# A mixture of experts in a fused last stage: gate and up with the weights stationary, router weights carried through memory

## The chip, the cores and the metric

The kernel runs on one core of a Trainium2 chip. The metric is device time in microseconds of one execution; the figure compared is the median of several runs. A core has five engines with queues of their own: TensorE (PE in the profile, its weight loads PEld), VectorE (DVE), ScalarE (ACT), GpSimd (POOL) and SyncE (SP), which here only issues DMAs. Each engine works through its own instruction queue in order and waits there for semaphores.

## The reference

Two layers of gated cross-attention and mixture of experts, on 32 sequences (B) of 256 tokens (S) with 256 features (D). The change lies in the second layer's mixture, the last part of the computation:

```python
# hidden_states: layernorm of the sequence, [B, 256, 256]; E = 8 experts, the first 4 with an MLP of I = 128
scores = sigmoid(x @ Wr)
_, idx = top_k(scores + router_bias, 2)
w = take_along_axis(scores, idx); w = w / (sum(w) + 1e-9)
cw = zeros((T, 8)).at[arange(T)[:, None], idx].add(w)
g = einsum('th,ehi->tei', x, Wg)
u = einsum('th,ehi->tei', x, Wu)
hid = silu(g) * u
mlp_out = einsum('tei,eih->teh', hid, Wd)
routed = einsum('te,teh->th', cw[:, :4], mlp_out)
routed += cw[:, 4:5] * x + cw[:, 6:7] * x + cw[:, 7:8] * relu(x)
shared = depthwise causal convolution of 4 taps over the sequence
return routed + shared        # then x + tanh(g_ffn[1]) * this
```

Everything is float32. Products that need it are split into a high and a low plane of a faster 32-bit format and run in three passes (`PASSES`: high by high, high by low, low by high); `split_product` writes them out.

## The kernel before

The program has stages: the first layer's attention, its routing and experts, and the last stage, the function `finish`, in which the change lies. `finish` works on one sequence of 256 tokens at a time, `b` in 0 to 31, as a software pipeline over steps `s` = 2 to 36. In step `s` the engines work on several batches at once: the gather and sum of the first layer's answers for batch `s` (`combine_first`, `combine_second`), the second layer's attention of `s - 2`, the norm and router of `s - 3`, the experts of `s - 4`, the closing sum of `s - 5`. Each engine has a function `step(s, p)`, in which the order of its work is written out by hand; nothing is reordered at run time, and semaphores named after what is ready (`hid_ok`, `total_ok`) tie the engines together. `at_least(eng, sem, n)` is the wait that protects a buffer from being overwritten early. `by_itself` puts an instruction of its own between waits.

The experts of one batch before the change. The 256 tokens are two tiles of 128 (`i` = 0, 1). PE makes `gates[i]` and `ups[i]` (`gate_up`) with the tokens of the tile as the stationary operand and the weights of the four experts (4 x 128 = 512 columns) moving, so the result has tokens on the partitions. ACT's `tanh` and DVE's `silu` make `hs`. DVE's `weigh` multiplies, in one fused operation for each expert, `hs` by the token's router weight, a scalar for each partition `cw[:, p, i, e]`, and by `ups`. PE turns the result (`turn_hid`, four transposes for each `i`), into the bank of `gates[i]`, since `down` needs the hidden features on the partitions. ACT's `hidden_turned` copies the high plane out, DVE's `hidden_low` makes the low plane, and PE's `down` sums the experts into `total`. `add_rest` adds the convolution `cv`, and DVE's `close` makes the output.

PE's order within step `s` before: `gate_up(s-4, 1, 0)`, `turn_c`, `down(s-5, 1)`, `values`, `add_rest(s-5, 1)`, `turn_hid(s-4, 0)`, `turn3`, `keys`, `gate_up(s-4, 1, 1)`, `turn4(s-3)`, `queries`, `turn_k`, `down(s-4, 0)`, `context`, `gate_up(s-3, 0, 0)`, `logits`, `attended`, `gate_up(s-3, 0, 1)`, `turn_hid(s-4, 1)`, `output`, `add_rest(s-4, 0)`. `gate_up(s-4, 1, 0)` waits, for the bank of `gates[1]`, until `hidden_low(s-5, 1)` is done.

DVE's order before: `weigh(s-4, 0)`, `stat4(s-3)`, `values_out`, `normalise4(s-3)`, `close(s-5)`, `hidden_low(s-4, 0)`, `key_max`, `silu(s-4, 1)`, four operations of `convolve`, `x4_lower(s-3)`, two more of `convolve`, `relu`, `own_heads`, `weigh(s-4, 1)`, `silu(s-3, 0)`, then `route_and_combine`: fifteen small router operations of batch `s-3` (semaphore `route`), between which stand `combine_first` and `combine_second` of batch `s`, `hidden_low(s-4, 1)` and `x3_new(s-2)`.

POOL's order: `shares(s-4)` (which waits for all of `route`), `keep_x2(s-2)` (it writes `f_x2k`), `norm4(s-3)` (which waits for `stat4` and writes `f_var`, `f_rs`), the gathers for batch `s`, `add_relu`, `norm3`. DVE's `normalise4` waits for `f_rs`.

The names in the profile carry the prefix `f_` for tiles of this stage. The lines that matter: L80 is every product of `split_product`, told apart by its tile; L2386 is `turn_hid`, L2379 `add_rest`, L2130 `weigh`, L2185 `hidden_low`, L2022 `hidden_turned`, L2179 `silu`, L2202 `x4_lower`, L2161 `normalise4`, L2153 `close`, L2197 `convolve`, L1930 `keep_x2`, L1939 and L1942 `norm4`, L1955 `shares`.

Of the kernel before, what the change touches and what calls it, by code (L numbers as in the profile page):

```python
# [31 lines left out]
P = 128  # L32
# [1726 lines left out]
def finish(nc, t, keep):  # L1759
# [4 lines left out]
    with ctx:  # L1764
# [8 lines left out]
        def sem(name):  # L1773
# [39 lines left out]
        cw = sb("f_cw", [P, 2, QT, E1])  # L1813
# [6 lines left out]
        hs = sb("f_hs", [P, QT, EM * P])  # L1820
        hid = sb("f_hid", [P, QT, EM * P])
        hidT = sb("f_hidT", [P, 2, QT, EM, P], F32R)
# [25 lines left out]
        hidT_low = [sem(f"f_hidT_low{i}") for i in range(QT)]  # L1848
        gate_made, up_made, th_ok, hs_ok, hid_ok, hid_made, hidT_ok, down_made, total_ok, yo_ok = (
            [sem(f"f_{s}{i}") for i in range(QT)] for s in (  # L1850
                "gate_made", "up_made", "th_ok", "hs_ok", "hid_ok", "hid_made", "hidT_ok", "down_made", "total_ok",
                "yo_ok"))
        yo_ok = yo_ok[0]
# [16 lines left out]
        def weight2(name, plane, k):  # L1870

            base = LATE_AT[name] - LATE_AT["Wg"]
            both = halves[:, plane, base:base + EM * KD * P].rearrange("p (e k i) -> p e k i", e=EM, k=KD)
            return both[:, :, k]

# [22 lines left out]
        @block.sync  # L1898
        def _(eng):
            def store(b, p):  # L1900
                eng.wait_ge(yo_ok, b + 1)
                eng.dma_start(t["out"][bass.ds(b, 1)].rearrange("o (k p) d -> p (o k) d", p=P), yo[:, p]) \
                    .then_inc(yo_out[p], 16)

            early["load_x1"](eng, 2, 0)

            def step(s, p):
                if live(s + 1):
                    early["load_x1"](eng, s + 1, 1 - p)
                if live(s):  # L1910
                    early["load_ctx"](eng, s, p)
                if live(s - 5):
                    store(s - 5, 1 - p)

            all_steps(eng, step)
            for p in range(2):
                eng.wait_ge(yo_out[p], 16 * (B // 2))

        @block.gpsimd
        def _(eng):  # L1920
# [26 lines left out]
            def shares(b, p):  # L1947


                eng.wait_ge(route, N_ROUTE * (b + 1))  # L1950
                eng.wait_ge(rg4_ok, b + 1)
                at_least(eng, x3p_ok, QT * b)
                at_least(eng, x4r_ok, QT * b)
                by_itself(eng, waited)
                nc.gpsimd.tensor_tensor(own[:, 0], cws[:], rg4[:], ALU.mult).then_inc(own_ok, 1)  # L1955
                nc.gpsimd.tensor_tensor(own[:, 3], cw[:, p, :, EM + 3], keep["gate"][:, 3:4].to_broadcast([P, QT]),
                                        ALU.mult).then_inc(own_ok, 1)
# [29 lines left out]
        def _(eng):  # L1987
# [23 lines left out]
            def first_tap(b):  # L2011

                eng.wait_ge(x4p_ok, b + 1)
                at_least(eng, total_ok[1], b)
# [70 lines left out]
            def step(s, p):  # L2085
# [6 lines left out]
                if live(s - 4):  # L2092
                    tanh(s - 4, 1)
                    first_tap(s - 4)
                    hidden_turned(s - 4, 0)
# [10 lines left out]
                if live(s - 3):  # L2106
                    x4_padded(s - 3)
                if live(s - 2):
                    queries_out(s - 2)
# [5 lines left out]
                if live(s - 4):  # L2115
                    hidden_turned(s - 4, 1)
# [4 lines left out]
        def _(eng):  # L2121
            def weigh(b, p, i):

                eng.wait_ge(hs_ok[i], b + 1)
                eng.wait_ge(up_made[i], b + 1)
                eng.wait_ge(route, N_ROUTE * (b + 1))
                at_least(eng, hid_made[i], b)
                for e in range(EM):
                    es = slice(e * P, (e + 1) * P)
                    nc.vector.scalar_tensor_tensor(hid[:, i, es], hs[:, i, es], cw[:, p, i, e:e + 1], ups[i][:, es],  # L2130
                                                   ALU.mult, ALU.mult).then_inc(hid_ok[i], 1)
# [16 lines left out]
            def close(b, p):  # L2148

                eng.wait_ge(total_ok[1], b + 1)  # L2150
# [31 lines left out]
            def hidden_low(b, i):  # L2182

                eng.wait_ge(hidT_ok[i], b + 1)
                nc.vector.scalar_tensor_tensor(hidT[:, 1, i], gates[i][:].rearrange("p (e s) -> p e s", e=EM), 0.5,  # L2185
                                               hidT[:, 0, i].bitcast(F32), ALU.mult, ALU.subtract) \
                    .then_inc(hidT_low[i], 1)
# [40 lines left out]
            def route_and_combine(b, p, c, cp):  # L2228
# [13 lines left out]
                at_least(eng, own_ok, N_OWN * b)  # L2242
                chain(nc.vector.tensor_scalar(re[:], re[:], 1.0, None, ALU.add))
# [31 lines left out]
                chain(nc.vector.tensor_tensor(cw[:, p], oh[:, :, 0], oh[:, :, 1], ALU.add))  # L2275
# [3 lines left out]
                chain(nc.vector.tensor_tensor(cw[:, p], cw[:, p], rsg[:], ALU.mult))  # L2279
# [3 lines left out]
                chain(nc.vector.reduce_sum(cws[:], cw[:, p], AX.X))  # L2283
# [7 lines left out]
                chain(nc.vector.tensor_tensor(cw[:, p], cw[:, p], wide(cws[:]), ALU.mult))  # L2291
                wait_chain()
                chain(nc.vector.tensor_tensor(cws[:], cw[:, p, :, EM], cw[:, p, :, EM + 2], ALU.add))
# [10 lines left out]

            def step(s, p):
                q = 1 - p
                if live(s - 4):
                    weigh(s - 4, p, 0)
# [14 lines left out]
                if live(s - 4):  # L2323
                    hidden_low(s - 4, 0)
                if live(s - 2):
                    key_max(s - 2)
                if live(s - 4):
                    silu(s - 4, 1)
                    convolve(s - 4, 1, KC - 1)
                if live(s - 3):  # L2330
                    x4_lower(s - 3)
                if live(s - 4):
                    convolve(s - 4, KC - 1, KC)
# [3 lines left out]
                if live(s - 4):  # L2337
                    weigh(s - 4, p, 1)
# [13 lines left out]
        def _(eng):  # L2352
# [8 lines left out]
            def down(b, i):  # L2361
                eng.wait_ge(hidT_low[i], b + 1)
                if i == 0:
# [3 lines left out]
                split_product(nc, total[:, i * D:(i + 1) * D], lambda a, e: hidT[:, a, i, e],  # L2367
                              lambda a, e: wd2[:, a, e], EM, stop=False).then_inc(down_made[i], 1)
# [5 lines left out]
            def add_rest(b, i):  # L2374

                if i == 0:
                    eng.wait_ge(cv_ok, N_CV * (b + 1))
                for k in range(KD):
                    last = nc.tensor.matmul(total[:, i * D + k * P:i * D + (k + 1) * P], cv[:, k, i * P:(i + 1) * P],  # L2379
                                            ident[:], is_transpose=True, start=False, stop=k == KD - 1)  # L2380
                last.then_inc(total_ok[i], 1)

            def turn_hid(b, i):
                eng.wait_ge(hid_ok[i], EM * (b + 1))
                for e in range(EM):
                    last = nc.tensor.transpose(gates[i][:, e * P:(e + 1) * P], hid[:, i, e * P:(e + 1) * P], ident[:])  # L2386
                last.then_inc(hid_made[i], 1)
# [46 lines left out]
            def gate_up(b, i, which):  # L2434

                out, name, done = ((gates, "Wg", gate_made), (ups, "Wu", up_made))[which]
                if which == 0:
                    eng.wait_ge(x4T_low, b + 1)
                    at_least(eng, hidT_low[i], b)
                else:  # L2440
                    at_least(eng, hid_ok[i], EM * b)
# [30 lines left out]
            def step(s, p):  # L2472
# [9 lines left out]
                if live(s - 5):  # L2482
                    add_rest(s - 5, 1)
                if live(s - 4):
                    turn_hid(s - 4, 0)
# [10 lines left out]
                if live(s - 4):  # L2496
                    down(s - 4, 0)
# [9 lines left out]
                if live(s - 4):  # L2507
                    turn_hid(s - 4, 1)
                if live(s - 2):
                    output(s - 2)  # L2510
                if live(s - 4):
                    add_rest(s - 4, 0)
# [4 lines left out]
def build(nc, t):  # L2517

    with ExitStack() as ctx:
# [24 lines left out]
        keep["w1_loaded"] = ctx.enter_context(nc.semaphore("w1_loaded"))  # L2544
        routing(nc, t, keep, ctx)
# [72 lines left out]
```

## Time and profile before

| | us |
|---|---|
| median of 3 runs | 2226.85 (2221.72 to 2227.82) |
| span of the profiled execution | 2225.1 |
| what the median lies above that span | 1.75 |
| busy in the whole span: PE, DVE, ACT, POOL | 2186.7, 1728.1, 1282.0, 645.1 |
| busy in 100 us of the last stage (1800 to 1900): PE, DVE, ACT, POOL | 100.00, 90.05, 55.85, 57.71 |

The last stage begins at about 1592 us; its steps 4 to 33 lie between 1631 and 2189 us. PE's busy time is modelled from the ends of pipelined matmuls, so a stretch in which PE is 100% busy can hold short waits. In the timelines an operation's length overlaps the next one's start a little, on DVE by some 0.08 us; what an operation costs in a row of others is the distance of the starts.

### The profile page before, as it was taken

The page shows a single profiled execution, that of the slowest core. Times are in us where ns is not written, and L with a number is a line of the kernel's source. Part 1 is how long each engine was busy: PE and PEld are TensorE (multiplying, and loading weights), DVE is VectorE, ACT ScalarE, POOL GpSimd, SP SyncE. Part 2 cuts the span into 40 slices and gives each one's busy share as a digit, 9 for nine tenths or more (in the row PEclk, how much of TensorE's full clock was granted, in tenths as well). Part 3 has the DMA queues.
Part 4 walks back from the last instruction along what each step waited for, and adds up shares of the span by engine and source line. Part 5 has one row for each costly group of instructions (what it writes and reads, how often), then busy time and mean ns, then how long its engine had stood idle before and what let it go on. Part 6 is the DMA issues. An engine that isn't in the chain of part 4 may idle for free. (4 is left out here: it accounts for less than half of the span.)

```text
span 2225.1 us, 48355 instructions
## 1 busy us (share of the span) xinstructions
PE 2186.7 (98%) x15486; PEld 1865.5 (84%) x15486; DVE 1728.1 (78%) x6112; ACT 1282.0 (58%) x3251; POOL 645.1 (29%) x1162
## 2 busy tenths in 40 slices
PE   8999999999999999999999999999999999999997
PEld 6777777777777777777699999999878888888886
DVE  6788888888888888888675555555579999999986
ACT  6776776776776776776443333433345555555553
POOL 1123223222232232232220000000355555555541
PEclk9999999999999999999899999999999999999999
DMA  5320110110110110110052222221212222222210
GB/s 189 124 97 22 37 40 23 37 39 21 40 38 20 39 39 20 40 32 27 11 161 73 81 86 72 81 77 41 89 58 65 65 65 64 65 65 65 65 39 20
DMA packets 111642, 129.57 MB, mean 58 GB/s; under 512 B 14898, under 2 KB 98089, under 8 KB 111264
## 3 DMA queue, kind: packets, MB, share of 16 engines
q1 hardware_dynamic: 98249, 105.06, 14.9%
q0 software_dynamic: 12288, 21.21, 3.3%
q8 instruction: 128, 2.10, 0.4%
q14 instruction: 122, 1.00, 0.1%
q10 hardware_dynamic: 855, 0.19, 0.0%
HBM read 84.26 MB, written 54.53 MB: 62 GB/s over the span
## 5 line engine op out<-in xcount | busy, mean ns | idle before, releaser
L711 ACT ACTIVATE a_prob<-a_prob,a_nmax 128x376 f32<-128x376 f32 x512 | 309.7, 606 | 155.3 <-DVE a_nmax L857 155.3
L1457 ACT ACTIVATE e_hidden<-e_first,keep_b 128x256 f32<-128x256 f32 x320 | 134.1, 471 | 283.3 <-PE e_first L80 282.8
L857 DVE CUSTOM_DVE_ANT_0 a_prob<-a_score,a_mask_row 128x376 f32<-128x376 f32 x512 | 266.6, 540 | 10.8 <-issue 5.6
L80 PE MATMUL e_second<-e_w,e_hidden 128*128 128x256 f32 x1920 | 239.5, 284 | 0.0
L80 PEld LDWEIGHTS e_second<-e_w,e_hidden 128*128 128x128 f32 x1920 | 232.6, 192 | 0.0
L869 DVE TENSOR_SCALAR a_prob<-a_prob,a_rden 128x376 f32<-128x376 f32 x512 | 220.9, 453 | 2.5
L1151 PE MATMUL a_turned<-keep_ident,a_prob 128*128 128x128 f32 (+1 forms) x1536 | 217.3, 277 | 2.8 <-DVE a_probT L876 1.6
L1151 PEld LDWEIGHTS a_turned<-keep_ident,a_prob 128*128 128x128 f32 (+1 forms) x1536 | 173.5, 142 | 43.5 <-issue 27.6
L1142 PE MATMUL a_score<-a_kT,a_qT 64*128 64x376 f32 x1024 | 196.4, 502 | 0.0
L876 DVE COPY a_probT<-a_turned 128x384 f32<-128x384 f32 x256 | 139.8, 546 | 54.4 <-PE a_turned L1151 54.4
L719 ACT ACTIVATE a_probT<-a_turned 128x384 f32<-128x384 f32 x256 | 124.9, 488 | 92.1 <-PE a_turned L1151 91.7
L177 POOL TENSOR_SCALAR r_var<-r_mv 128x2 f32<-128x2 f32 x64 | 12.2, 190 | 562.9 <-issue 501.2
L201 POOL DMA_INDIRECT slots<-r_x2h,r_sidx x128 | 134.4, 1050 | 77.0 <-DVE keep_row L332 46.5
L80 PE MATMUL a_work<-a_wkv,a_kvin 128*128 128x512 f32 (+1 forms) x576 | 154.3, 403 | 1.4 <-DVE a_att L881 1.4
L1178 PE MATMUL a_work<-a_probT,a_vo 128*64 128x256 f32 (+1 forms) x1152 | 148.4, 393 | 2.6 <-ACT r_rT L217 1.9
L1695 POOL DMA_INDIRECT w_in<-answers,o_row x128 | 132.9, 1038 | 58.7 <-issue 31.0
L1178 PEld LDWEIGHTS a_work<-a_probT,a_vo 128*64 128x64 f32 (+1 forms) x1152 | 75.4, 138 | 81.6 <-issue 50.2
L1504 DVE CAST e_hidden<-e_hidden 128x512 fp32r<-128x512 f32 x160 | 68.5, 428 | 96.8 <-ACT e_hidden L1457 96.6
L1142 PEld LDWEIGHTS a_score<-a_kT,a_qT 64*128 64x128 f32 x1024 | 88.1, 186 | 50.4 <-issue 18.4
L1690 POOL COPY o_row<-keep_row 128x4 uint32<-128x4 uint32 x32 | 10.0, 313 | 412.3 <-DMA answers<-e_y 412.3
L80 PEld LDWEIGHTS a_work<-a_wkv,a_kvin 128*128 128x128 f32 (+1 forms) x576 | 101.6, 186 | 20.8 <-issue 1.5
L80 PE MATMUL e_first<-e_rowsT,keep_w 128*128 128x256 f32 x960 | 118.8, 282 | 0.0
(237 smaller groups left out, 5231.1 us busy)
## 6 DMA issues: line engine op xcount, KB each, us to landing
w_in<-W SPq DMA_DIRECT2D x32, 512.0 KB, 4.1
slots<-a_zeros SPq DMA_DIRECT2D x8, 1280.0 KB, 8.7
keep_rows<-slots SPq DMA_DIRECT2D x40, 256.0 KB, 3.9
answers<-e_y SPq DMA_DIRECT2D x40, 256.0 KB, 2.2
a_xn<-x SPq DMA_DIRECT2D x32, 256.0 KB, 2.9
a_xr<-x SPq DMA_DIRECT2D x32, 256.0 KB, 3.8
x<-r_x SPq DMA_DIRECT2D x32, 256.0 KB, 4.0
w_in<-x SPq DMA_DIRECT2D x32, 256.0 KB, 2.6
```

The costliest lines, as they stand in the source:

```text
L80: last = nc.tensor.matmul(out, stationary(a, t), moving(b, t), start=start and n == 0, stop=stop and n == len(todo) - 1)
L201: nc.gpsimd.indirect_dma_start(out=t["slots"], out_offset=bass.IndirectOffsetOnAxis(ap=sidx[:, p, n:n + 1], axis=0), in_=x2h[:, p, n // 2] ...
L711: nc.scalar.activation(prob[:, u % 4, a], prob[:, u % 4, a], ACT.Exp, bias=nmax[:, u % 4, a:a + 1], scale=-1.0, accum_out=den[:, u % 4, a: ...
L719: nc.scalar.activation(probT[:, u // 2 % 2, a, :, u % 2 * P:(u % 2 + 1) * P], turned_keys[a], ACT.Copy) \
L857: nc.vector.tensor_tensor_reduce(prob[:, u % 4, a], score[SCORE_AT[u][a]][:, 0:NKV], mask_row[:, p], -1.0, 3.0e38, ALU.add, ALU.min, nmax[ ...
L869: nc.vector.tensor_scalar(prob[:, u % 4, a], prob[:, u % 4, a], rden[:, u % 4, a:a + 1], None, ALU.mult) \
L876: nc.vector.tensor_copy(probT[:, u // 2 % 2, a, :, u % 2 * P:(u % 2 + 1) * P], turned_keys[a]) \
L1142: nc.tensor.matmul(score[SCORE_AT[u][a]][:, 0:NKV], qT[rows, p, m, i * P:(i + 1) * P], kT[rows, p, m], start=True, stop=True).then_inc(sco ...
L1151: last = nc.tensor.transpose(turned_keys[a][0:hi - lo, j], prob[:, u % 4, a, lo:hi], ident[:])
L1178: last = nc.tensor.matmul(out[64 * a:64 * a + 64, 0:S], vo[0:hi - lo, p, j, m, a], probT[0:hi - lo, m % 2, a, j], start=j == 0, stop=j == 2)
L1457: nc.scalar.activation(hidden[:, 2 * j + i], first[:, j, i * CH:(i + 1) * CH], ACT.Relu, bias=b1[:, 2 * j + i, bass.ds(e, 1)]).then_inc(re ...
L1695: nc.gpsimd.indirect_dma_start(out=picked[p][:, n], out_offset=None, in_=t["answers"][0:rows], in_offset=bass.IndirectOffsetOnAxis(ap=row[ ...
```

## The change

Gate and up are made with the weights as the stationary operand and all 256 tokens moving, so their results have the hidden features on the partitions, and the tiles are now pairs of experts (`j` = 0, 1; `gates[j]` and `ups[j]` hold two experts of 256 tokens). The transposes `turn_hid` fall away. A token's router weight is then no longer a scalar for each partition: the weights are turned by DVE in blocks of 32, written to a DRAM tensor `chosen` by four small stores, and read back by one DMA that gives every partition all 1024 of them (`cw_wide`). `weigh` becomes `share_ups` (up times router weight) and `hidden` (times `hs`). `down` sums by expert pairs, `add_rest` comes in one piece.

```diff
+        cwp = sb("f_cwp", [P, 2, 32])
+        cw = [cwp[:, n, 0:QT * E1].rearrange("p (e i) -> p i e", i=QT) for n in range(2)]
+        cw_rows = sb("f_cw_rows", [P, 32])
+        cw_wide = sb("f_cw_wide", [P, EM, S])
...
+            def spread_weights(b):                      # SP, first in step s, for b = s - 4
+                eng.wait_ge(cw_turned, b + 1)
+                for g in range(0, P, 32):
+                    eng.dma_start(t["chosen"][:, g:g + 32], cw_rows[g:g + EM * QT]).then_inc(cw_out, 16)
+                eng.wait_ge(cw_out, 16 * 4 * (b + 1))
+                at_least(eng, share_ok[1], b)
+                eng.dma_start(cw_wide[:].rearrange("p e s -> p (e s)"),
+                              t["chosen"].rearrange("c q -> (c q)").partition_broadcast(P)).then_inc(cw_in, 16)
...
-            def hidden_turned(b, i):                    # ACT
-                eng.wait_ge(hid_made[i], b + 1)
-                at_least(eng, down_made[i], b)
-                nc.scalar.activation(hidT[:, 0, i], gates[i][:].rearrange("p (e s) -> p e s", e=EM), ACT.Copy,
-                                     scale=0.5).then_inc(hidT_ok[i], 1)
+            def hidden_high(b, j):
+                eng.wait_ge(hid_ok[j], b + 1)
+                at_least(eng, down_made[j], b)
+                nc.scalar.activation(hid2[:, 0, pair(j)], hid[:, j].rearrange("p (e s) -> p e s", e=2), ACT.Copy,
+                                     scale=0.5).then_inc(hid_high[j], 1)
...
-            def weigh(b, p, i):                         # DVE
-                eng.wait_ge(hs_ok[i], b + 1)
-                eng.wait_ge(up_made[i], b + 1)
                 eng.wait_ge(route, N_ROUTE * (b + 1))
-                at_least(eng, hid_made[i], b)
-                for e in range(EM):
-                    es = slice(e * P, (e + 1) * P)
-                    nc.vector.scalar_tensor_tensor(hid[:, i, es], hs[:, i, es], cw[:, p, i, e:e + 1], ups[i][:, es],
-                                                   ALU.mult, ALU.mult).then_inc(hid_ok[i], 1)
+                at_least(eng, cw_out, 16 * 4 * b)       # weights_turned(b, p)
+                nc.vector.transpose(cw_rows[:], cwp[:, p]).then_inc(cw_turned, 1)
+
+            def share_ups(b, j):
+                eng.wait_ge(up_made[j], b + 1)
+                eng.wait_ge(cw_in, 16 * (b + 1))
+                at_least(eng, hid_low[j], b)
+                nc.vector.tensor_tensor(hid[:, j].rearrange("p (e s) -> p e s", e=2),
+                                        ups[j][:].rearrange("p (e s) -> p e s", e=2), cw_wide[:, pair(j)],
+                                        ALU.mult).then_inc(share_ok[j], 1)
+
+            def hidden(b, j):
+                eng.wait_ge(hs_ok[j], b + 1)
+                eng.wait_ge(share_ok[j], b + 1)
+                nc.vector.tensor_tensor(hid[:, j], hs[:, j], hid[:, j], ALU.mult).then_inc(hid_ok[j], 1)
...
+            def down(b, j):                             # PE
+                eng.wait_ge(hid_low[j], b + 1)
+                for i in range(QT):
+                    for n, (a, c, e) in enumerate((a, c, 2 * j + e) for e in range(2) for a, c in PASSES):
+                        last = nc.tensor.matmul(total[:, i * D:(i + 1) * D], hid2[:, a, e, i * P:(i + 1) * P],
+                                                wd2[:, c, e], start=j == 0 and i == 0 and n == 0, stop=False,
+                                                skip_group_check=True)
...
             def gate_up(b, j, which):
                 if which == 0:
                     eng.wait_ge(x4T_low, b + 1)
-                    at_least(eng, hidT_low[i], b)
+                    at_least(eng, hs_ok[j], b)
                 else:
-                    at_least(eng, hid_ok[i], EM * b)
-                split_product(nc, out[i][:].rearrange("p (e i) -> p e i", e=EM),
-                              lambda a, k: x4T[:, a, k, i * P:(i + 1) * P],
-                              lambda a, k: weight2(name, a, k), KD).then_inc(done[i], 1)
+                    at_least(eng, share_ok[j], b)
+                for e in range(2):
+                    last = split_product(nc, out[j][:, e * S:(e + 1) * S], lambda a, k: weight2(name, a, k)[:, 2 * j + e],
+                                         lambda a, k: x4T[:, a, k], KD)
```

The notes behind `#` in this diff name the engine or the function; they are not in the code. The orders after the change, where they differ:

- DVE: `weights_turned(s-4)` stands where `weigh(s-4, 0)` stood. `hidden_low(s-4, 0)` leaves its place before `key_max`. `share_ups(s-4, 0)` stands behind the four operations of `convolve` and before `x4_lower`, `hidden(s-4, 0)` behind `x4_lower`. Where `weigh(s-4, 1)` stood come `share_ups(s-4, 1)`, `hidden(s-4, 1)` and `hidden_low(s-4, 0)`. `hidden_low(s-4, 1)` stays among the router's operations. The last of these writes the weights into `cwp`, which DVE clears once at the start of the stage.
- ACT: `hidden_high(s-4, 0)` stands behind `x4_padded` (`hidden_turned(0)` stood behind `first_tap`), `hidden_high(s-4, 1)` at the end.
- PE: no `turn_hid`; `down(s-4, 0)` at the end of the step, behind `output`, instead of between `turn_k` and `context`; `add_rest(s-5)` in one piece where `add_rest(s-5, 1)` stood.
- SP: `spread_weights(s-4)` ahead of `load_x1(s+1)`, `load_ctx(s)` and `store(s-5)`.

## Rows read from the trace of the kernel before

**Rows 1.** The page, busy time of each engine over the whole span.

```profile
PE 2186.7 (98%) x15486; PEld 1865.5 (84%) x15486; DVE 1728.1 (78%) x6112; ACT 1282.0 (58%) x3251; POOL 645.1 (29%) x1162
```

**Rows 2.** Chain of waits, last stage: start, length (us), what.

```profile
2116.59 0.19 POOL f_var L1939
...
2132.55 0.61 DVE f_hidT L2185
```

**Rows 3.** Timeline of PE: start, length, line, tile, count [idle before].

```profile
1908.85 1.62 PE L80 MATMUL f_gates<-late,f_x4T 128*128 128x512 f32 x6
...
1910.44 1.68 PE L80 MATMUL f_total<-f_wd,f_hidT 128*128 128x256 f32 x12
...
1913.04 0.60 PE L2386 MATMUL f_gates<-keep_ident,f_hid 128*128 128x128 f32 x4
1913.47 0.60 PE L2394 MATMUL f_bank_x<-keep_ident,f_x3h 128*128 128x128 f32 x4
...
2133.30 1.62 PE L80 MATMUL f_gates<-late,f_x4T 128*128 128x512 f32 x6 [2.19 <-DVE f_hidT L2185]
...
2151.78 1.62 PE L80 MATMUL f_gates<-late,f_x4T 128*128 128x512 f32 x6
...
2170.22 1.63 PE L80 MATMUL f_gates<-late,f_x4T 128*128 128x512 f32 x6
...
2217.66 2.93 PE L80 MATMUL f_total<-f_wd,f_hidT 128*128 128x256 f32 x12 [0.98 <-DVE f_hidT L2185]
```

**Rows 4.** Timeline of DVE: one steady step, and the last batch's first `weigh`.

```profile
1892.09 1.12 DVE L2130 SCALAR_TENSOR_TENSOR f_hid<-f_hs,f_cw,f_ups 128x128 f32<-128x128 f32 x4 [0.21 <-DVE f_cws L2293]
...
1895.80 0.74 DVE L2161 TENSOR_SCALAR f_x4h<-f_x,f_mv,f_rs 128x256 f32<-128x256 f32 x2 [0.84 <-POOL f_rs L1942]
...
1900.63 0.68 DVE L2202 TENSOR_TENSOR f_x4T<-keep_bank,f_x4T 128x512 fp32r<-128x512 f32 x1
1901.23 0.86 DVE L2197 SCALAR_TENSOR_TENSOR f_cv<-f_x4p,o_conv_w,f_cv 128x256 f32<-128x256 f32 x2
...
1903.32 1.11 DVE L2130 SCALAR_TENSOR_TENSOR f_hid<-f_hs,f_cw,f_ups 128x128 f32<-128x128 f32 x4
1904.35 0.68 DVE L2179 SCALAR_TENSOR_TENSOR f_hs<-f_th,f_gates 128x512 f32<-128x512 f32 x1
...
1910.57 1.12 DVE L2130 SCALAR_TENSOR_TENSOR f_hid<-f_hs,f_cw,f_ups 128x128 f32<-128x128 f32 x4 [0.21 <-DVE f_cws L2293]
...
2206.04 1.12 DVE L2130 SCALAR_TENSOR_TENSOR f_hid<-f_hs,f_cw,f_ups 128x128 f32<-128x128 f32 x4 [0.23 <-DVE f_cws L2293]
```

**Rows 5.** Timeline of POOL in the same step.

```profile
1892.08 0.20 POOL L1955 TENSOR_TENSOR f_own<-f_cws,f_rg 128x2 f32<-128x2 f32 x1 [4.54 <-DVE f_cws L2293]
...
1892.92 1.28 POOL L1930 TENSOR_TENSOR f_x2k<-w_in,o_bo 128x512 f32<-128x512 f32 x1
1894.52 0.19 POOL L1939 TENSOR_SCALAR f_var<-f_mv 128x2 f32<-128x2 f32 x1 [0.32 <-DVE f_mv L2141]
```

**Rows 6.** Timeline of DVE in the stage of the experts.

```profile
1121.67 0.43 DVE L1504 CAST e_hidden<-e_hidden 128x512 fp32r<-128x512 f32 x1 [0.28 <-ACT e_hidden L1457]
1122.13 0.69 DVE L1506 TENSOR_TENSOR e_hidden<-e_hidden 128x512 fp32r<-128x512 f32 x1
```

**Rows 7.** Timeline of SP's queue: issues in a row.

```profile
1128.22 0.47 SPq L1403 DMA_DIRECT2D late<-WkT  x1
1128.73 0.47 SPq L1403 DMA_DIRECT2D late<-WvT  x1
```

**Rows 8.** DMA issues: count, KB each, median us from issue to landing.

```profile
w_in<-W SPq DMA_DIRECT2D x32, 512.0 KB, 4.1
...
out<-f_yo SPq DMA_DIRECT2D x32, 256.0 KB, 2.2
...
r_slot<-slot SPq DMA_DIRECT2D x1, 128.0 KB, 6.7
a_go<-g_o SPq DMA_DIRECT2D x1, 128.0 KB, 6.4
```

More of the change, by code:

```diff
@@ L1955, in shares @@
                 nc.gpsimd.tensor_tensor(own[:, 0], cws[:], rg4[:], ALU.mult).then_inc(own_ok, 1)
-                nc.gpsimd.tensor_tensor(own[:, 3], cw[:, p, :, EM + 3], keep["gate"][:, 3:4].to_broadcast([P, QT]),
+                nc.gpsimd.tensor_tensor(own[:, 3], cw[p][:, :, EM + 3], keep["gate"][:, 3:4].to_broadcast([P, QT]),
                                         ALU.mult).then_inc(own_ok, 1)
@@ L2107, in step @@
                     x4_padded(s - 3)
+                if live(s - 4):
+                    hidden_high(s - 4, 0)
                 if live(s - 2):
@@ L2115, in step @@
                 if live(s - 4):
-                    hidden_turned(s - 4, 1)
+                    hidden_high(s - 4, 1)
             all_steps(eng, step)
@@ L2274, in route_and_combine @@
                 wait_chain()
-                chain(nc.vector.tensor_tensor(cw[:, p], oh[:, :, 0], oh[:, :, 1], ALU.add))
+                chain(nc.vector.tensor_tensor(cw[p], oh[:, :, 0], oh[:, :, 1], ALU.add))
                 if low:
@@ L2278, in route_and_combine @@
                 wait_chain()
-                chain(nc.vector.tensor_tensor(cw[:, p], cw[:, p], rsg[:], ALU.mult))
+                chain(nc.vector.tensor_tensor(cw[p], cw[p], rsg[:], ALU.mult))
                 if combining:
@@ L2302, in x3_new @@
                                                keep["gate"][:, 1:2], x2k[:], ALU.mult, ALU.add).then_inc(x3_ok, 1)
+            nc.vector.memset(cwp[:], 0.0).then_inc(cw_set, 1)
             def step(s, p):
@@ L2329, in step @@
                     convolve(s - 4, 1, KC - 1)
+                    share_ups(s - 4, 0)
                 if live(s - 3):
@@ L2332, in step @@
                 if live(s - 4):
+                    hidden(s - 4, 0)
                     convolve(s - 4, KC - 1, KC)
@@ L2337, in step @@
                 if live(s - 4):
-                    weigh(s - 4, p, 1)
+                    share_ups(s - 4, 1)
+                    hidden(s - 4, 1)
+                    hidden_low(s - 4, 0)
                 if live(s - 3):
@@ L2372, in values, with add_rest @@
                 product(bank_c[0:C, 0:D], lambda k: cT[:, k], lambda k: weight("WvT", k), KD).then_inc(v_made, 1)
[L2374 to L2387, printed above, removed]
+            def add_rest(b):
+                eng.wait_ge(cv_ok, N_CV * (b + 1))
+                for i in range(QT):
+                    for k in range(KD):
+                        last = nc.tensor.matmul(total[:, i * D + k * P:i * D + (k + 1) * P],
+                                                cv[:, k, i * P:(i + 1) * P], ident[:], is_transpose=True, start=False,
+                                                stop=i == QT - 1 and k == KD - 1, skip_group_check=True)
+                last.then_inc(total_ok, 1)
             def turn3(b):
@@ L2432, in context, with gate_up @@
                 last.then_inc(cx_made, 1)
-            def gate_up(b, i, which):
+            def gate_up(b, j, which):
                 out, name, done = ((gates, "Wg", gate_made), (ups, "Wu", up_made))[which]
@@ L2482, in step @@
                 if live(s - 5):
-                    add_rest(s - 5, 1)
-                if live(s - 4):
-                    turn_hid(s - 4, 0)
+                    add_rest(s - 5)
                 if live(s - 2):
@@ L2511, in step @@
                 if live(s - 4):
-                    add_rest(s - 4, 0)
+                    down(s - 4, 0)
             all_steps(eng, step)
```

65 lines of the change are left out of this document (31 added, 34 removed).

## Prediction

> **What bounds the kernel now.** I read the page's busy shares first. TensorE (PE) shows 98% [rows 1], which suggests that any PE work taken away is time gained. The chain of waits says otherwise. In the piece of it that lies in the last stage it runs through a whole step on VectorE (DVE), goes through GpSimd's (POOL) variance instructions and comes back to DVE [rows 2]. It reaches PE only from `hidden_low` (L2185). So I went to the timelines of a steady step.
>
> PE's next `gate_up` cannot start before DVE has made the low half of the previous batch. When DVE was held up once, PE stood idle for 2.19 us with exactly that releaser [rows 3]. DVE's step, from one first `weigh` to the next, is 1910.57 - 1892.09 = 18.48 us [rows 4]. PE's own step is shorter. It shows where DVE has no gather left to combine: 2170.22 - 2151.78 = 18.44 us [rows 3]. PE therefore looks full because its own length happens to be 0.04 us under DVE's. In a steady step DVE waits for nothing that PE makes: it stands before `weigh` for its own router result, and 0.84 us before `normalise4` for POOL's `rs4` [rows 4]. **DVE, with POOL in its loop, sets the pace, and PE is close behind.**
>
> **The change, part by part.**
>
> *PE.* The two `turn_hid` go: 1913.47 - 1913.04 = 0.43 us each, 0.86 per step. Gate and up become 12 products of 256 columns instead of 6 of 512. `down` already is twelve of 256: 1.68 us beside 1.62 for a gate group of six [rows 3], so four groups cost 4 x 0.06 = 0.24 more. PE's own work falls by about 0.6 us to some 17.8. `down(0)` used to stand between `turn_k` and `context` and covered ScalarE's (ACT) copy of the keys. Now PE must wait for that copy, under 1 us. All of this lies beside DVE's longer step and is worth nothing on the path. If DVE weren't the limit, the 0.6 would come off each step and the wait would give it back. `add_rest` in one piece costs the same four transposes; `total` is ready early for `close`.
>
> *ACT.* `hidden_high` is the same 128x512 copy as `hidden_turned`. It moves in the queue behind `x4_padded`, ahead of `queries_out`; DVE feeds it 0.6 us after the operation that feeds `x4_padded`, so what waits behind it (`queries_out`, `tanh(0)`) is late by about one such copy, which DVE's longer stretch before `silu(0)` covers.
>
> *DVE, busy.* Out: eight `weigh` operations of 128x128, in two groups of 1904.35 - 1903.32 = 1.03 us each, -2.06. In: two `share_ups` and two `hidden`, each a tensor_tensor of 128x512. The row of that kind in this stage, `x4_lower` with one operand in PSUM, takes 1901.23 - 1900.63 = 0.60 us start to start [rows 4]; with both operands in SBUF it is as long, 0.69 for one [rows 6]. Four make +2.40. `hidden(1)` directly follows `share_ups(1)`, on which it depends. A dependent pair starts 0.03 us after the first has ended (1121.67 + 0.43 to 1122.13, [rows 6]), instead of overlapping it by 0.08: +0.11. `hidden_low` reads SBUF instead of PSUM and stays at 0.61 [rows 2]. In sum 2.40 + 0.11 - 2.06 = +0.45. The reason: one fused operation with three operands becomes two with two, so twice the elements pass.
>
> The Trainium skill ("VectorE: DVE Perf Modes", Rules for kernel authors) advises to minimize the number of operations. By that rule, taken by itself, eight becoming four would halve the 2.06 to 1.03, and the sum of all would end near 2227. The rows go the other way, since the elements outweigh the starts saved: 2.06 against 2.40.
>
> *DVE, where the first group stood.* The first `weigh` stood between the router and `stat4`. The transpose of 128x32 that takes its place has no row; it lies between nothing and one 128x512 operation (0.69), and either is hidden, for this reason: `normalise4` waits for POOL, and POOL's variance instruction stands in POOL's queue behind `shares` and `keep_x2`, which start at the router's end. POOL starts `shares` at 1892.08 and `keep_x2` at 1892.92, which takes 1.28 and ends at 1894.20. Today the variance starts at 1894.52 [rows 5]. With `stat4` a microsecond earlier, POOL can start it only at about 1894.2, so `normalise4` moves from 3.71 us after the step's start (1895.80 - 1892.09) to about 3.40. Of 1.03 us removed here only 0.31 is gained; the remaining 0.72 becomes a longer wait for POOL. Bounds: 0.2 (POOL needs the same latency again) and 1.03 (POOL is not in the way).
>
> *One step then:* +2.40 + 0.11 - 1.03 (second group) - 0.31 (first group) = **+1.17 us**, 19.65 in place of 18.48. Bounds by the ends above: +0.45 and, with 0.69 for each of the four, +1.64.
>
> *The router weights through memory.* They travel: transpose on DVE, four stores by SyncE (SP), a wait, one broadcast of 512 KB, and `share_ups(0)` waits for it. The slot of `share_ups(0)` is that of today's `x4_lower` (1900.63 - 1895.80 = 4.83 us behind `normalise4`), less the `hidden_low(0)` that leaves this stretch (0.6), so 3.40 + 4.83 - 0.60 = 7.63 us after the step's start. SP issues in a row start 0.51 us apart [rows 7]; the fourth starts at 0.2 + 1.53 = 1.73. A store lands in at most 2.2 us (256 KB), a 512 KB load in 4.1 [rows 8]. Upper end: 1.73 + 2.2 + 4.1 = 8.0; lower, if a small store took nothing, 5.8. For stores this small I take 1.7, so 7.5: just in time, with 0.1 us per step set aside for gathers on the same engines. A broadcast reads one place 128 times; the nearest rows, a broadcast and a plain load of 128 KB side by side at the start, took 6.4 and 6.7 us [rows 8], so it isn't slower by itself. Behind SP's two waits stand `load_x1`, `load_ctx` and `store`. They leave some 4 us into the step; the loads are used one or two steps later, and the `yo` buffer is two deep, so nobody waits.
>
> *Ends.* 28 steps (4 to 31, as long as there is something to combine) bear the full sum. In steps 32 and 33 DVE is lighter and PE sets the pace; its gain of 0.6 and its new wait cancel: 0. Step 34 bears the DVE sum without POOL's part: +1.5. In the last batch the broadcast is not covered: `share_ups(0)` at 7.5, then seven DVE operations of some 0.6 to 0.8 up to the last low half at about 12.5, two `down` as long as today's last one (2.93 us after a gap, [rows 3]), `add_rest`, `close` and the store: about 23 us, where today it is 19.1 from 2206.04 [rows 4] to the span's end at 2225.1: +4. The tail: +5 (1.5 to 6). The single stall of 2.19 us came by a late gather, which has more time now: -1. The memset of `cwp`, once: nothing.
>
> *Sum:* 28 x (1.17 + 0.1) = 35.6; + 5 - 1 = +39.6. Span 2225.1 + 39.6 = 2264.7 us. The median of the runs (2226.85) lies 1.75 above the profiled span; within the rounding of my terms I say **2265**.
>
> **The rivals.**
>
> *A, PE sets the pace (other side).* For it: the 98%. Against it: the 2.19 us wait and 18.44 under 18.48. It would need DVE's new step to be under PE's 17.8, so 1.9 us less than my sum. Then 30 steps x 0.6 to 0.75 come off, and the tail gives some back: about 2207.
>
> *B, the broadcast is late.* Its landing decides, from 7.63 us on; each microsecond later costs 28 us. At 9 us: 2264 + 36 = 2300. For it: only 0.1 us of margin, and gathers run at that time. Against it: the rows' upper end is 8.0 (+10 us).
>
> *C, POOL is not in the way.* The first `weigh` counts in full: +0.45 per step, 28 x 0.45 + 4 = +17: 2242.
>
> *D, nothing measurable.* DVE's two groups of two large operations cost no more than the eight small ones did, so that only POOL's wait and the tail are left, and both are small: 2227. For it: the number of operations falls by half. Against it: 0.60 for one large operation beside 1.03 for four small ones [rows 4]. The Trainium skill's rule above ends here.
>
> **How the numbers follow.** My case 0.52, B (2275 or more) 0.20, C 0.11, A 0.09, D 0.08. My own case lies within 2250 to 2275. The range for 8 in 10 takes in C and the larger part of B: 2238 to 2297. A measurement here can tell about 0.3% (7 us): faster 0.10, same 0.07, slower 0.83.
>
> **What would show it.** Right: a DVE step of 19.5 to 19.8 us; PE with waits of half a microsecond before `context`, `gate_up(0)` and `attended`, busy some 90%; an `f_x4h` wait for `f_rs` that has grown above 1 us; `share_ups(0)` with little wait for the DMA. Wrong: a DVE that waits for PE (A), an `f_x4h` wait no longer than before (C), a wait of a microsecond or more at `share_ups(0)` (B), or tensor_tensors much under 0.6 us.

## The result and the profile after

The changed kernel takes **2267.18 us** (median of 4 runs, 2263.54 to 2272.03) beside 2227.25 us (four runs) of the kernel before on the same chip: a ratio of 1.0182 [1.0164, 1.0200], so 40 us or 1.8% slower. The forecast was 2265. The profiled execution is the longest of the four: it took 2272.03 us, its span is 2270.2, so its sum stands some 5 us above the median.

The page's busy line of the changed kernel, over the whole span:

```profile
PE 2191.1 (97%) x15998; PEld 1891.2 (83%) x15998; DVE 1745.8 (77%) x6017; ACT 1271.8 (56%) x3251; POOL 678.7 (30%) x1162
```

The busy times in a stretch of the last stage (start and end; length; busy us of PE, its weight loads, DVE, ACT and POOL; then the granted clock, the DMA share and GB/s):

```profile
1800.00:1900.00 100.00, 92.71 (x661) 85.50 (x660) 86.80 (x292) 48.15 (x116) 57.88 (x96) 1.00 0.29 88
```

Against [rows 1], where PE had 98%, nothing seems to have moved. In the stretch PE went from 100.00 to 92.71 and DVE from 90.05 to 86.80: both are less busy, in a step that is longer. So there are waits. The two lists of waits (waiting engine, tile and line; releaser; us in total, times, longest), from 1750 to 2100:

```profile
DVE f_v L2174 <- PE f_bank_c L1886: 19.0, 18, 1.1
DVE f_x4h L2189 <- POOL f_rs L1959: 16.3, 18, 1.1
...
DVE f_hid L2151 <- issue: 0.8, 3, 0.4
...
PE f_bank_c L1886 <- ACT f_kp L2066: 8.5, 18, 0.5
PE keep_bank L1886 <- ACT f_x4p L2072: 7.1, 17, 0.4
PE f_bank_x L1886 <- ACT f_qT L2079: 4.8, 17, 0.3
PE f_gates L80 <- DVE f_x4T L2230: 2.7, 7, 0.6
```

PE waits before `context` and `attended`, as forecast, before `gate_up(0)` in 7 of 18 steps, and also before `logits`, which the forecast didn't name. DVE waits 0.9 us for POOL's `f_rs`, about as long as before ([rows 4], 0.84), and now 1.1 us for PE's `values` ahead of it. At `share_ups(0)` (L2151) it hardly waits for the broadcast: three times in 18 steps, by 0.4 us at most. The list gives these three as `issue`; each ends 0.1 us after a late broadcast has landed.

The timeline of DVE in one undisturbed step, the counterpart of [rows 4], then POOL's of the same step, the counterpart of [rows 5], then SP's queue:

```profile
1772.30 0.21 DVE L2144 STREAM_TRANSPOSE f_cw_rows<-f_cwp 128x32 f32<-128x32 f32 x1
...
1774.66 0.42 DVE L2174 TENSOR_TENSOR f_v<-f_bank_c,o_bv 120x256 f32<-120x256 f32 x1 [1.10 <-PE f_bank_c L1886]
1775.97 0.74 DVE L2189 TENSOR_SCALAR f_x4h<-f_x,f_mv,f_rs 128x256 f32<-128x256 f32 x2 [0.89 <-POOL f_rs L1959]
...
1780.19 0.68 DVE L2151 TENSOR_TENSOR f_hid<-f_ups,f_cw_wide 128x512 f32<-128x512 f32 x1
1780.79 0.68 DVE L2230 TENSOR_TENSOR f_x4T<-keep_bank,f_x4T 128x512 fp32r<-128x512 f32 x1
1781.39 0.68 DVE L2159 TENSOR_TENSOR f_hid<-f_hs,f_hid 128x512 f32<-128x512 f32 x1
1781.99 0.88 DVE L2225 SCALAR_TENSOR_TENSOR f_cv<-f_x4p,o_conv_w,f_cv 128x256 f32<-128x256 f32 x2
...
1784.08 0.68 DVE L2151 TENSOR_TENSOR f_hid<-f_ups,f_cw_wide 128x512 f32<-128x512 f32 x1
1784.86 0.69 DVE L2159 TENSOR_TENSOR f_hid<-f_hs,f_hid 128x512 f32<-128x512 f32 x1
1785.47 0.68 DVE L2213 SCALAR_TENSOR_TENSOR f_hid<-f_hid 128x512 fp32r<-128x512 f32 x1
...
1792.13 0.21 DVE L2144 STREAM_TRANSPOSE f_cw_rows<-f_cwp 128x32 f32<-128x32 f32 x1
```

```profile
1772.47 0.20 POOL L1972 TENSOR_TENSOR f_own<-f_cws,f_rg 128x2 f32<-128x2 f32 x1 [5.01 <-DVE f_cws L2323]
...
1773.32 1.28 POOL L1947 TENSOR_TENSOR f_x2k<-w_in,o_bo 128x512 f32<-128x512 f32 x1
1774.68 0.19 POOL L1956 TENSOR_SCALAR f_var<-f_mv 128x2 f32<-128x2 f32 x1
...
1783.55 1.27 POOL L1984 TENSOR_TENSOR f_x3p<-f_x3p,f_x4r 128x512 f32<-128x512 f32 x1 [0.60 <-DVE f_x4r L2238]
```

```profile
1772.54 1.29 SPq L1916 DMA_DIRECT2D chosen<-f_cw_rows  x4
1774.71 0.35 SPq L1919 DMA_DIRECT2D f_cw_wide<-chosen  x1
```

DVE's step is 1792.13 - 1772.30 = **19.83 us** in place of 18.48: +1.35. The four new operations cost 0.60, 0.60, 0.78 and 0.61 us from start to start, 2.59 in sum, for the 2.06 of the eight removed. POOL's variance (L1956) comes right behind `keep_x2`, without the idle time of [rows 5]. From POOL's first `shares` to `normalise4` it is 1775.97 - 1772.47 = 3.50 us, where it was 1895.80 - 1892.08 = 3.72 [rows 4, 5]. So of the 1.03 us taken away ahead of `stat4`, 0.22 came through. 2.59 - 1.03 - 0.22 = 1.34: the step is explained.

### The profile page after: what moved, and what is told of

Same layout as the page of the kernel before. It is cut to its first block and busy times, and to the rows that moved or that the text cites. A ratio compares the mean times of both kernels' runs of the same rounds, so it can differ in the third digit from the quotient of the medians.

```text
span 2270.2 us, 49509 instructions
## 1 busy us (share of the span) xinstructions
PE 2191.1 (97%) x15998; PEld 1891.2 (83%) x15998; DVE 1745.8 (77%) x6017; ACT 1271.8 (56%) x3251; POOL 678.7 (30%) x1162
## 5 line engine op out<-in xcount | busy, mean ns | idle before, releaser
L1695 POOL DMA_INDIRECT w_in<-answers,o_row x128 | 147.2, 1150 | 58.7 <-issue 30.7
L2403 PE MATMUL f_total<-f_wd,f_hid 128*128 128x256 f32 x768 | 113.0, 298 | 6.9 <-DVE f_hid L2213 6.9
```

The costliest lines, as they stand in the source:

```text
L1695: nc.gpsimd.indirect_dma_start(out=picked[p][:, n], out_offset=None, in_=t["answers"][0:rows], in_offset=bass.IndirectOffsetOnAxis(ap=row[ ...
```

## The experiments

Each ratio is against the kernel before on the same chip. Steps are distances of DVE's starts in undisturbed steps.

**Who sets the pace.** `e3_no_share` takes the two `share_ups` out of the changed kernel.

```diff
-                    share_ups(s - 4, 0)
...
-                    share_ups(s - 4, 1)
                     hidden(s - 4, 1)
...
-                nc.vector.tensor_tensor(hid[:, j], hs[:, j], hid[:, j], ALU.mult).then_inc(hid_ok[j], 1)
+                nc.vector.tensor_tensor(hid[:, j], hs[:, j], ups[j][:], ALU.mult).then_inc(hid_ok[j], 1)
```

> The changed kernel without the two share_ups: hidden multiplies hs by ups straight from PSUM, so the router weights are left out of the sum; the trip through memory and the wait for it stay. Theory (DVE sets the pace): two operations of 0.60 us and the dependent wait of 0.19 go, the step becomes 18.45 us, 28 x 1.39 = 39 us less, about 2228, unless PE with its new waits becomes the limit on the way, at 18.5 to 19 us (2230 to 2244). Rival (PE sets the pace): unchanged, 2267.

Measured: 2226.33 us, ratio 1.0002 [0.9992, 1.0012], some 40 us below the changed kernel, though PE's work and the trip through memory are left in. So the loss hangs on DVE's work. Its lists of waits, same columns and stretch as above:

```profile
DVE f_v L2176 <- PE f_bank_c L1886: 35.0, 19, 1.9
...
PE f_bank_c L1886 <- ACT f_kp L2066: 9.0, 19, 0.5
```

The step is 18.48. DVE now waits 1.8 us for PE in each step (35.0 in 19), and PE hardly for anything but ACT's key copy: PE sets the pace there, with some 18.0 of its own and 0.47 of that wait. That this equals the step before is chance, and it puts a floor under the change that the forecast's rival A, with 2207, didn't have.

`e4_before_pe`, `e5_before_dve` and `e6_before_both` relieve the kernel before of PE work, of DVE work, and of both:

```diff
-                split_product(nc, out[i][:].rearrange("p (e i) -> p e i", e=EM),       # e4, e6
...
+                todo = [(a, c, k) for k in range(KD) for a, c in PASSES[:2]]
...
-        N_CV = KD * (KC - 1)                                                           # e5, e6
+        N_CV = KD * (KC - 2)
...
-                    convolve(s - 4, KC - 1, KC)
```

> The kernel before with two of the three passes of gate and up; the third, low by high, is left out. PE's work falls by 8 products of 512 columns, 1.85 us per step; DVE's work is the same. Theory (DVE sets the pace at 18.48): the steps stay, steps 32 and 33 and the tail give 4 to 7 us, 2220 to 2223. Rival (PE sets the pace at 98% busy): 30 x 1.85 = 55 us less, 2172.

> The kernel before without the last tap of its convolution, which is left out: VectorE has two operations of 128x256 fewer per step, some 0.8 us; TensorE has the same work. Theory (VectorE 18.48 and TensorE 18.44 are within 0.04 of each other, so relief of one alone gives nothing): 2220 to 2225 us. Rival (VectorE alone sets the pace, with TensorE's 18.44 containing waits that shrink): 28 x 0.8 = 22 us less, 2203.

> The kernel before with both reliefs: the last tap of the convolution and the third of the three passes of the gate and up products are left out, so VectorE has 0.8 us less per step and TensorE 1.85. Theory: the step falls to VectorE's 17.7, 28 x 0.8 = 22 us and some 4 at the ends: 2197 to 2203. Rival (something third, ScalarE or the DMA, holds the step at 18.4): 2218 to 2225.

Measured: 2222.52 (0.9989 [0.9976, 1.0002], step 18.48), 2220.95 (0.9971 [0.9960, 0.9981], step 18.44) and 2207.27 (0.9903 [0.9886, 0.9919], steps of 17.7 to 18.3). 1.85 us less PE work gives nothing in a step, 0.8 less DVE work gives the 0.04 by which DVE was longer (28 x 0.04 = 1 us; the other 5 I didn't follow), and only both together shorten the step. The tie of [rows 3, 4] is real. The last gain is 20 us where I had 24 to 30, since the step came down only here and there to 17.7; what held the others I didn't follow.

**The trip through memory.** `e2_no_trip` leaves out the turning, the stores, the broadcast and the wait for it.

```diff
-                if live(s - 4):
-                    spread_weights(s - 4)
...
-                eng.wait_ge(cw_in, 16 * (b + 1))
+                eng.wait_ge(cw_set, 2)
```

> The changed kernel without the trip of the router weights through memory: cw_wide is set to one once, SP sends nothing for it, so the router weights are left out of the sum over the experts; all of PE's and DVE's work stays (the transpose too). Theory (DVE's own operations make the step, the trip is nearly covered): the steps stay at 19.83, only the few late broadcasts (2.4 us in all) and 2 to 4 us of the tail come off, 2260 to 2264. Rival (the trip or its 512 KB on the DMA engines make the step longer): 20 us or more come off, 2245 or less.

Measured: 2262.96 (1.0176 [1.0158, 1.0194]). By the ratios this is 1.3 us below the changed kernel, within the intervals, and an undisturbed step is 19.81 in place of 19.83. The trip is nearly covered: the broadcast is issued 2.41 us behind the transpose and takes 4.3 (median), so it lands 6.7 behind, 1.2 ahead of `share_ups(0)` at 7.89. In the three steps with a wait it was issued 2.9 to 3.5 behind and landed 8.0 to 8.3 behind.

**The wait for POOL.** If `keep_x2` holds `norm4` back, swapping them should give the step 0.9 us.

```diff
-                if live(s - 2):
-                    keep_x2(s - 2, p)
                 if live(s - 3):
                     norm4(s - 3)
+                if live(s - 2):
+                    keep_x2(s - 2, p)
```

> The changed kernel with norm4 ahead of keep_x2 in POOL's order; nothing is left out. Theory (DVE sets the pace, and the place of the first weigh is lost to a wait for POOL's norm behind keep_x2): f_var starts about 1.1 us earlier, the step falls from 19.83 by 0.7 to 0.9 us, so 28 x 0.8 = 22 us less than the changed kernel, about 2245. Rival (PE's new waits for ACT set the step): the step stays at 19.8, about 2267.

Measured: 2273.33 (1.0216 [1.0199, 1.0233]), step 19.91: a miss for the theory. DVE's and POOL's timelines of `e1_norm_first`:

```profile
1773.79 0.21 DVE L2144 STREAM_TRANSPOSE f_cw_rows<-f_cwp 128x32 f32<-128x32 f32 x1
...
1776.56 1.70 DVE L2189 TENSOR_SCALAR f_x4h<-f_x,f_mv,f_rs 128x256 f32<-128x256 f32 x2
...
1776.75 1.35 POOL L1947 TENSOR_TENSOR f_x2k<-w_in,o_bo 128x512 f32<-128x512 f32 x1
```

`normalise4` has no wait ahead of it any more and starts 2.77 us behind the transpose instead of 3.67, 0.90 earlier. But its two operations take 1.70 us instead of 0.74: they run into `keep_x2` and get done about when it is. To tell this from a limit of PE, `e7_x2_last` put `keep_x2` behind `add_relu`, and `e10_x2_dve` gave it to DVE:

```diff
-                    keep_x2(s - 2, p)                  # POOL; norm4 follows shares
...
+                    keep_x2(s - 2, p)                  # e7: POOL, behind add_relu; e10: DVE, ahead of values_out
```

> The kernel after, with GpSimd's order changed: norm4 directly behind shares, and the 128x512 addition keep_x2 moved behind the gather and add_relu, so that it runs neither ahead of f_var nor beside the normalise4 operations. Nothing is left out. Theory (the wait for f_rs costs the step 0.9 us; the run with norm4 ahead of keep_x2 lost its gain because the two normalise4 operations stood beside keep_x2, 1.70 us against 0.74): normalise4 starts 2.8 us behind the transposes instead of 3.67 and takes 0.74; DVE's step falls from 19.83 to about 18.95, some 28 x 0.9 = 25 us: 2242 us, 2238 to 2252. Rival (TensorE's order and its waits for ScalarE, 17.8 of its own and 1.2 of waits, hold the step as well): the step stays above 19.5 and the time above 2258.

> The kernel after, with keep_x2 (the 128x512 addition of the bias to x2) taken from GpSimd and given to VectorE, right ahead of f_v, where VectorE waits 1.1 us for TensorE; norm4 then follows shares directly. Nothing is left out. Theory (in the kernel after, keep_x2 holds norm4 back, and wherever else GpSimd ran it, one of VectorE's operations stood beside it for 1.0 us; on VectorE it is some 0.6 us in a hole of 1.1): normalise4 starts 2.8 us behind the transposes instead of 3.67 and takes 0.74; the step falls from 19.83 to about 19.0; 28 x 0.85 = 24 us: 2243 us, 2238 to 2255, the upper end if the broadcast, which lands 6.7 us behind the transposes, is now waited for before share_ups(0), at 7.0. Rival (TensorE's order holds the step): above 2258.

Measured: 2286.14 (1.0263 [1.0246, 1.0281]), a miss, and 2252.29 (1.0115 [1.0092, 1.0138]). In `e7_x2_last` the collision has moved to `hidden(1)`, which takes 1.73 us instead of 0.69:

```profile
1788.78 1.27 POOL L1947 TENSOR_TENSOR f_x2k<-w_in,o_bo 128x512 f32<-128x512 f32 x1
...
1788.86 1.73 DVE L2159 TENSOR_TENSOR f_hid<-f_hs,f_hid 128x512 f32<-128x512 f32 x1
```

On top `share_ups(0)` comes earlier there and waits for the broadcast (ten times from 1750 to 2100, up to 1.3 us). In `e10_x2_dve` the operation is a DVE one in a place where DVE waits anyhow, and nothing collides:

```profile
1768.92 0.66 DVE L2140 TENSOR_TENSOR f_x2k<-w_in,o_bo 128x512 f32<-128x512 f32 x1
1769.94 0.42 DVE L2171 TENSOR_TENSOR f_v<-f_bank_c,o_bv 120x256 f32<-120x256 f32 x1 [0.36 <-PE f_bank_c L1886]
1770.72 0.73 DVE L2186 TENSOR_SCALAR f_x4h<-f_x,f_mv,f_rs 128x256 f32<-128x256 f32 x2 [0.35 <-POOL f_rs L1950]
```

The step is 19.13 in most steps: -0.70. The time ends in the upper part of what was expected, since `f_v` and `f_rs` are still waited for, 0.5 and 0.2 us on average. So the theory holds in a changed form: POOL's place in the loop costs 0.7 us a step by `e10_x2_dve`, 0.9 by the start of `normalise4` in `e1_norm_first`, but in both other places that were tried POOL's 1.28 us cost more than they gave back.

**Can the loss be ordered away?** `e8_order` is e7 with `silu(1)` moved ahead of `f_v` and the weighings moved; `e9_all_orders` is e10 with the orders of DVE, ACT and PE changed; `e11_pe_order_back` is e9 with the PE edit taken back; `e12_x4h_act` is e11 with `normalise4` given to ACT and PE's `queries` in two halves. The cores of the edits:

```diff
+                    silu(s - 4, 1)                     # DVE, behind stat4 (e8, e9, e11, e12)
...
+                    share_ups(s - 4, 1)                # between the reciprocal of f_ksum and f_cx (the same)
...
+                    queries_out(s - 2)                 # ACT, ahead of hidden_high(0) (e9, e11, e12)
...
+                    gate_up(s - 4, 1, 1)               # PE, behind turn_k (e9 alone)
...
+                    nc.scalar.activation(x4h[:, p, i], x3[:, p, i], ACT.Identity, scale=rs4[:, i:i + 1],
+                                         bias=sh4[:, i:i + 1]).then_inc(x4h_ok, 1)       # e12
...
+                    queries(s - 2, 0)                  # PE (e12)
+                    turn_k(s - 2)
+                    queries(s - 2, 1)
```

> The run above, with VectorE's order changed too: silu(1) put into the wait ahead of f_v (1.1 us), the weighing of ups 0 behind x4_lower, the weighing of ups 1 between the reciprocal of f_ksum and f_cx (into a gap of 0.44 us, and away from the dependent hidden(1), 0.19). Nothing is left out. Theory (each of these gaps is on VectorE's path): 0.35 + 0.63 less than the run above for VectorE, 18.0; TensorE then sets the pace with 17.8 of its own and 0.5 of the wait for f_kp, 18.3 to 18.6; 28 x 1.3 = 36 us below the kernel after: 2231 us, 2222 to 2240. Rival (the gaps are filled by something else that is late, the broadcast above all, since share_ups(0) comes 6.8 us behind the transposes here and the broadcast lands 6.7 behind): waits before share_ups(0), the time no better than the run above.

> The run above, with the orders of the three engines changed too: VectorE's silu(1) ahead of f_v, the two weighings later and away from the products that use them; ScalarE's tanh(1) ahead of normalise3 and queries_out ahead of hidden_high(0); TensorE's ups(1) between turn_k and context, where it waits 0.47 us for f_kp. Nothing is left out. Theory (the change costs VectorE 0.45 us of work per step and 0.9 of waits, and the waits can be ordered away): VectorE has some 18.2 us of work without waits, TensorE 17.9; a step of 18.3 to 18.6: 2218 to 2232 us, as long as the kernel before. Rival (the waits only move to other places): 2240 or more.

> The run e9_all_orders with one of its edits taken back: TensorE's ups(1) is again ahead of turn4. Nothing is left out. In e9 x4_turned of ScalarE waited up to 2.1 us for ups(1), which still reads the one f_x4T, and VectorE's x4_lower up to 2.5 us for x4_turned. Theory (only that edit was wrong; the other orders take the waits away): no wait of VectorE before x4_lower; VectorE some 18.2 us of work, TensorE 17.9 and 0.5 of the wait for f_kp; a step of 18.4 to 18.7, 28 x 1.2 = 34 us below the kernel after: 2222 to 2238 us. Rival (the weighings' later place or ScalarE's orders cost as well): 2245 or more, as the run with keep_x2 on VectorE alone or slower.

> The run e11_pe_order_back, with the two normalise4 operations taken from VectorE to ScalarE (scale and shift, the shift made by one more 128x2 operation of GpSimd), behind f_xT in its order, x3_own behind keys_turned, and TensorE's queries in two halves with turn_k between them. Nothing is left out. Theory (VectorE sets the pace in e11 with a step of 18.72, of which normalise4 is 0.65 and its wait for f_rs 0.43): VectorE has 17.7 us per step; TensorE then sets it with 17.9 and without the wait of 0.47 for f_kp: a step of 18.0 to 18.2, 28 x 0.6 = 17 us below e11: 2217 us, 2210 to 2225, below the kernel before. Rival (ScalarE's queue is late: f_x4h comes 5.4 us behind the transposes, when TensorE's turn4 wants it, and f_x4T behind it): waits of TensorE and VectorE for ScalarE, 2228 or more.

Measured: 2265.41 (1.0180 [1.0162, 1.0198]), 2300.74 (1.0333 [1.0314, 1.0352]), 2234.51 (1.0026 [1.0015, 1.0038]) and 2224.15 (0.9981 [0.9972, 0.9989]).

- `e8_order` missed: in it `hidden_low(0)` stands beside `keep_x2` and takes 1.77 instead of 0.68, and the waits for `f_th` (0.46) and for the broadcast (up to 1.0) are new.
- `e9_all_orders` missed by far, for one edit. The list of waits names it: ups(1) reads the one `f_x4T`, so ACT may not write the next one until ups(1) is done, and `x4_lower` waits behind.

```profile
DVE f_x4T L2229 <- ACT f_x4T L2049: 35.8, 16, 2.5
...
ACT f_x4T L2049 <- PE f_ups L80: 32.1, 16, 2.1
```

- `e11_pe_order_back` has a step of 18.72, with one regular wait of DVE for another engine left, 0.4 for `f_rs`. Its time is in the expected range.
- `e12_x4h_act` has a step of 18.38 where 18.0 to 18.2 was expected; its time is at the upper end of its range. PE waits 0.31 for DVE's `f_cx`, DVE 0.65 for PE's `keys`, and `hidden(1)` stands beside `add_relu` (1.09 us for 0.68). It is some 43 us below the changed kernel and 0.2% below the one before, so with the new layout of the experts the program can be as fast as before, once DVE is relieved elsewhere. Whether the kernel before would gain from the same moves wasn't tried, so this doesn't say that the layout itself costs nothing.

## Why the prediction was right, step by step

- **The bound** was right: DVE sets the pace, PE 0.04 behind (e4, e5, e6).
- **PE**: the 0.6 us less is nearer 0.45 (18.0 of its own in e3), and the wait for the key copy (0.47) gives all of it back. The 0.24 added for the smaller products isn't there: from start to start the four gate and up groups of a step take 5.95 us in e3 and 5.97 in the kernel before. My 0.06 compared the lengths of `down` and of a gate group, not their starts. Here both lie beside DVE's longer step, as predicted. For rival A the term mattered, and its 2207 was too low.
- **DVE, busy**: predicted +0.45, measured 2.59 - 2.06 = +0.53. The dependent `hidden(1)` starts 0.78 behind `share_ups(1)`, where I had 0.71: 0.10 after its end, not 0.03. The advice of the Trainium skill ("VectorE: DVE Perf Modes", Rules for kernel authors), given there for chained operations, to minimize their number doesn't hold here as a measure of time: the 4 took 0.53 us more than the 8, and the runs with and without `share_ups` show that DVE's time is on the path.
- **The place of the first group**: predicted 0.31 gained, measured 0.22, the lower bound almost. POOL's variance starts where forecast, right behind `keep_x2`. "POOL is in the way" was right; that one could take it out of the way by order alone (my theory for e1) was wrong.
- **The signs**: two of those named spoke against the forecast. DVE waits 1.1 us for PE ahead of `f_v`, which was to speak for A; and the wait for `f_rs`, which was to grow above 1 us, stayed at 0.9, hardly longer than before, which was to speak for C. But `f_v` ends at 1775.08, and `normalise4` still has to wait for POOL until 1775.97, so PE's lateness doesn't set that start, and e3 speaks against A. A wait that is spent ahead of `f_v` isn't listed again behind it. Both signs were ill chosen; the distance from `shares` to `normalise4` is the one to read.
- **The step**: predicted 19.65 and 0.1 for the trip, measured 19.83. DVE's busy time was 0.08 too small and the gain of the first group 0.09 too large. The trip takes 0.02 of an undisturbed step (e2), so the 0.1 set aside for it covered half of these errors by luck. What it costs in the disturbed steps lies within the spread of the runs.
- **The trip**: predicted to land at 7.5 for a slot at 7.63, measured 6.7 and 7.89. The landing time that I allowed the small stores was too long: the four are issued within 1.29 us, and SP issues the broadcast 0.9 us after the last was issued. Rival B had less behind it than the 0.20 I gave it, though the broadcast landed behind 7.89 in three steps of 18.
- **Ends**: from the start of the last batch to the end of the span, predicted +4, measured (2270.2 - 2248.1) - 19.06 [rows 4] = +3.0. The row of all transposes, with their first and last start:

```profile
L2144 DVE STREAM_TRANSPOSE f_cw_rows<-f_cwp x32: 211/212/217, 1633.5 to 2248.1; 128x32 f32<-128x32 f32 x32
```

  Of the 45.1 us between the two spans 28 x 1.35 = 37.8 are the lengthening of an undisturbed step, 3.0 the last batch, and the remaining 4.3 the disturbed steps (up to 21.76 us) and the last three: the one-off gain of 1 us didn't come. My sum was 5 us under this execution and 2 under the median.

## What to carry to other kernels

Price a rewrite on VectorE by the elements that pass, with starts of like operations from the trace, and not by the number of operations: one fused operation with a per-partition scalar does what two tensor-by-tensor operations do. When two engines are tied, what a change adds to the longer one counts, while relief of either alone is worth next to nothing (here 0.1% and 0.3%). Before an operation of GpSimd is moved out of the way, look at which VectorE operation it will then stand beside.

## What the runs showed of the hardware

A 128x512 addition of GpSimd from SBUF stops some VectorE operations that run at the same time, not all. Beside `keep_x2`, `normalise4` took 1.70 us instead of 0.74 and `hidden(1)` 1.73 instead of 0.69; both read and write SBUF alone. Beside `add_relu`, of the same size, `share_ups(1)` of the changed kernel keeps its 0.68 (1784.08, `add_relu` from 1783.55 to 1784.82): one of its operands is in PSUM. The loss, 0.96 and 1.04, is a little less than the 1.2 us that were left of GpSimd's operation. It also goes the other way. In `e11_pe_order_back` `hidden(0)` starts 0.17 us ahead of `add_relu` and keeps its 0.67, and `add_relu` takes 1.63 instead of 1.27:

```profile
1792.74 0.67 DVE L2158 TENSOR_TENSOR f_hid<-f_hs,f_hid 128x512 f32<-128x512 f32 x1
...
1792.91 1.63 POOL L1975 TENSOR_TENSOR f_x3p<-f_x3p,f_x4r 128x512 f32<-128x512 f32 x1 [0.25 <-DVE f_x4r L2237]
```

The Trainium skill ("SBUF — State Buffer", SBUF: two separate sides) says that the two engines share a port pair, that the one that starts first holds it for the whole instruction, and that VectorE needs it in its two-port modes or, against a GpSimd operation that reads SBUF, with two SBUF inputs; the rows of `hidden` and `share_ups` agree. `normalise4` has one tensor input, and in which mode it runs no row shows.

A transpose of 128x32 on VectorE takes 0.21 us, and the broadcast of 512 KB that reads one small place for every partition lands after 4.3 us (median), about as long as a load of that size before the change [rows 8]. What I hadn't counted is that it delays the others on the same queue. Their issues (count, KB each, median us to landing) were these, first in the changed kernel, then in `e2_no_trip`:

```profile
w_in<-x SPq DMA_DIRECT2D x32, 256.0 KB, 4.8
out<-f_yo SPq DMA_DIRECT2D x32, 256.0 KB, 3.9
...
w_in<-x SPq DMA_DIRECT2D x32, 256.0 KB, 2.7
out<-f_yo SPq DMA_DIRECT2D x32, 256.0 KB, 2.2
```

Without the trip they are as short as before (2.2 for the store, [rows 8]). The lists of waits name neither of them, as forecast.
